# Key sums of a linear-attention and mixture-of-experts kernel: the halves of the key products added on GpSimd, 16 transposed blocks in place of 32, and other slots for the steps

## The reference

```
x = x + layernorm(attn(layernorm(x)))
x = x + layernorm(ffn(layernorm(x)))

def attn(x):                       # 16 heads of 16
    xn = rms(x, g1)
    Q, K, V = xn @ Wq.T, xn @ Wk.T, xn @ Wv.T
    pQ, pK = elu(Q), elu(K)
    Q1, Q2 = split(pQ, 2);  K1, K2 = split(pK, 2)
    kv1 = einsum('bshe,bshd->bsed', K1, V) * SCALE     # sum over the 16 HEADS of one position
    kv2 = einsum('bshe,bshd->bsed', K2, V) * SCALE
    attn = Q1 kv1 - lmb * Q2 kv2
    attn = (1 - LAMBDA_INIT) * rms(attn, g2)
    attn = rms(attn, g3) + attn
    return gelu(attn @ W1.T) @ W2.T + attn

def ffn(h):                        # 16 query heads, 4 key heads, causal softmax attention, RoPE
    h = h + softmax_attention(rms(h)) @ Wo ; clip
    top 2 of 8 experts by softmax(rms(h) @ Wr), each silu(h Wg) * (h Wu) @ Wd, width 512
    clip(h + weighted sum of the experts)
```

## Time and profile before

| | us |
|---|---|
| median of 3 runs | 3368.0 |
| lowest, highest | 3363.05, 3370.25 |
| profiled execution, its own time | 3372.2 |
| its span | 3370.3 |
| busy: TensorE, VectorE, ScalarE, GpSimd | 2875.5, 2161.4, 1670.3, 1732.7 |

### The profile page before, as it was taken

How to read it: one execution, slowest core, us unless ns; L and a number is a source line. 1 busy time by engine, 2 the same in 40 slices (tenths; PEclk the granted TensorE clock), 3 DMA queues, 4 the chain that set the end, 5 groups by cost and what they waited for, 6 DMA issues and landing times. The chain is left out here.

```text
span 3370.3 us, 54068 instructions
## 1 busy us (share of the span) xinstructions
PE 2875.5 (85%) x17348; PEld 1707.3 (51%) x17349; DVE 2161.4 (64%) x4652; ACT 1670.3 (50%) x3836; POOL 1732.7 (51%) x2301
## 2 busy tenths in 40 slices
PE   4566899899989889989988998988759999999990
PEld 3344545554545554554555454443336666666650
DVE  3566887888898888888888888667322222222226
ACT  1234657667657656666765765765412222222224
POOL 5686746765765865776676575241212222222221
PEclk8788999999999999999999999999779999999995
DMA  1000000000000000000000000002243333333326
GB/s 46 0 10 10 11 9 14 14 25 12 27 22 14 28 20 17 22 19 23 17 22 27 12 24 19 12 25 81 73 112 53 57 58 57 58 52 58 58 43 200
DMA packets 102670, 123.21 MB, mean 37 GB/s; under 512 B 14384, under 2 KB 90160, under 8 KB 102448
## 3 DMA queue, kind: packets, MB, share of 16 engines
q1 hardware_dynamic: 76720, 85.54, 8.6%
q0 software_dynamic: 25728, 34.88, 6.0%
HBM read 58.23 MB, written 61.36 MB: 35 GB/s over the span
## 5 line engine op out<-in xcount | busy, mean ns | idle before, releaser
L822 ACT ACTIVATE wd<-SP_ 128x512 f32<-128x512 f32 (+3 forms) x1536 | 722.9, 488 | 477.9 <-PE SP_ L1439 334.0
L1105 DVE TENSOR_REDUCE NM<-MX 128x1 f32<-128x512 f32 (+3 forms) x1216 | 763.6, 655 | 243.9 <-PE MX L1396 145.2
L1393 PE MATMUL MX<-KST,QST 96*128 96x512 bf16 (+3 forms) x1536 | 457.5, 336 | 101.5 <-DVE NM L1105 89.2
L509 POOL TENSOR_TENSOR wg<-wu 128x1024 f32<-128x1024 f32 x256 | 487.4, 1924 | 106.3 <-DVE wu L941 106.2
L1436 PE MATMUL SP_<-QST,KST 99*128 99x512 bf16 (+3 forms) x1536 | 500.9, 333 | 34.3 <-ACT wd L822 15.8
L1718 POOL DMA_INDIRECT scratch_h<-Y,XG x136 | 211.2, 1553 | 604.5 <-DVE Y L1781 511.1
L1759 DVE TENSOR_TENSOR AG<-UB,SL 128x512 f32<-128x512 f32 x136 | 94.1, 692 | 460.3 <-PE UB L1798 456.9
L1736 ACT ACTIVATE SL<-GB 128x512 f32<-128x512 f32 x136 | 81.2, 597 | 603.4 <-PE GB L1798 603.4
L954 DVE TENSOR_TENSOR wg<-wu,SUM 128x1024 f32<-128x1024 f32 x256 | 310.4, 1213 | 99.7 <-PE SUM L1290 99.7
L1393 PEld LDWEIGHTS MX<-KST,QST 96*128 96x128 bf16 x1536 | 135.7, 98 | 433.9 <-DVE NM L1105 303.5
L1453 PE MATMUL OA<-wd,V 128*32 128x512 f32 (+3 forms) x3072 | 332.7, 506 | 1.0 <-ACT wd L822 0.4
(11 more groups left out here) (244 smaller groups left out, 4974.0 us busy)
## 6 DMA issues: line engine op xcount, KB each, us to landing
XG<-scratch_xs SPq DMA_DIRECT2D x136, 130.0 KB, 2.1
wu<-in_L_attn_x SPq DMA_DIRECT2D x64, 128.0 KB, 2.1
scratch_x<-wu SPq DMA_DIRECT2D x64, 128.0 KB, 1.7
scratch_h<-H SPq DMA_DIRECT2D x64, 128.0 KB, 1.7
X<-scratch_x SPq DMA_DIRECT2D x16, 512.0 KB, 4.0
HH<-scratch_h SPq DMA_DIRECT2D x16, 512.0 KB, 4.8
out<-X SPq DMA_DIRECT2D x16, 512.0 KB, 3.2
wg<-in_L_ffn_Wg SPq DMA_DIRECT2D x8, 512.0 KB
```

The costliest lines, as they stand in the source:

```text
L509: sg["prod1"].by(pool.tensor_tensor(P1[:, k // 2, (k % 2) * hh * D:(k % 2 + 1) * hh * D].rearrange("p (h e d) -> p h e d", h=hh, e=HD), QK ...
L822: sg["exp"].by(act.activation(PR[:, n % 8, q0:512], SP_[:, n % 2, q0:512], ACT.Exp))
L1105: sg["mx"].by(dve.tensor_reduce(NM[:, u % 2, part, i, h:h + heads], MX[:, index % 2, 0:heads * n].rearrange("p (h n) -> p h n", n=n), AX.X ...
L1393: m = pe.matmul(out[:, k], QST[0:MROW, j % 2, g * G + h + k, i * P:(i + 1) * P], KST[0:MROW, keys % RK, g, 0:n], start=k == 0, stop=not la ...
```

## The change

GpSimd adds the two quarters of each half of P1 in place as soon as both are there: the second 1024 floats are added to the first 1024. TensorE then has 4 heads' worth of blocks per half, 16 blocks per tile. The count `prod1` goes up by 6 per tile, not 4, and its users follow. Beside this many steps stand in other slots, the scatters are tied to slots 7, 15, 20 and to slot 2 of the next period, and LATE and AHEAD of the short units are 2.2 and 7.9 in place of 2.5 and 9.2. `share` and `LAST_BACK` are written in another way and give the same numbers.

```diff
-        LATE, AHEAD, DONE, SPREAD = (2.5, 1.6), (9.2, 6.2), (2.0, 3.0), (3.5, 8.5)
+        LATE, AHEAD, DONE, SPREAD = (2.2, 1.6), (7.9, 6.2), (2.0, 3.0), (3.5, 8.5)
...
@@ SyncE
-                        if i == 4 and p >= 0 and have(p + 3):
-                            load(p + 3)
-                        if i == 14 and have(p - 17):
-                            t = p - 17
+                        if i == 4 and have(p - 18):
+                            t = p - 18
...
-                        if i == 19 and have(p - 6):
+                        if i == 21 and have(p - 6):
...
+                        if i == 21 and have(p + 3):
+                            load(p + 3)
...
@@ GpSimd, key_products
+                    if k % 2 == 1:
+                        need("prod1", 6 * t + 3 * (k // 2) + 2)
+                        half = P1[:, k // 2]
+                        sg["prod1"].by(pool.tensor_tensor(half[:, 0:hh * D], half[:, 0:hh * D], half[:, hh * D:2 * hh * D], ALU.add))
...
+                def spread(k, n):
+                    t = CH * (k // CH) + 2 * (k % CH) + n // 2
+                    scatter(t, n % 2)
...
@@ GpSimd, the table
-                        if i == 2 and have(p - 1):
+                        if i == 1 and have(p - 1):
                             head_roots(p - 1)
...
+                        if i == 15 and have(p + 2):
+                            x_coefficients(p + 2)
...
-                        if i == 19 and have(p + 2):
-                            x_coefficients(p + 2)
...
@@ VectorE
-                        if i == 21 and (p - 21) % CH == 0 and have(p - 21):
-                            choose((p - 21) // CH)
+                        if i == 0 and (p - 22) % CH == 0 and have(p - 22):
+                            choose((p - 22) // CH)
...
@@ TensorE, sum_heads
-                    need("prod1", 4 * t + 2 + 2 * half)
-                    hh = H // 2
+                    need("prod1", 6 * t + 3 + 3 * half)
+                    hh = H // 4
```

## The result

The changed kernel takes 3497.6 us in the median of four runs (3495.4 to 3499.8), the kernel before 3367.4 on the same chip: a ratio of 1.039, interval 1.0373 to 1.0406. That is 130 us slower, and above the range of 3280 to 3385. The profiled execution has a span of 3497.9 us, 127.6 more than before.

A forecast was written before the change was run, and what follows sets the result against it. TensorE's own queue, with VectorE close behind, was taken to bound the steady part, and GpSimd the part before 290 us. Steady -51 and early +24 gave -27 us: 3341 us on the median, 0.8% faster, range 3280 to 3385.

The forecast's parts named there:

- Where GpSimd idles more than 4.44 us per stretch the work lies beside TensorE's: Steady part: two additions per tile, 4.44 us, cost nothing where GpSimd has that much idle time in a stretch.
- The addition's price: On GpSimd: one addition of 1024 elements takes 2.22 us, between 1.92 and 2.89, so 4.44 us per tile.
- the slower rival: GpSimd leads with additions of 2.9 us; early and tight stretches lengthen, steady gain halves to 25: 3398 us, chance 0.21.
- The tight three stretches: Neighbouring stretches, 828.4 to 918.5 us, where GpSimd would take the lead: 89.3 us against 90.1, counted as 0.
- The five others of the round: Steady stretches outside the tight three: TensorE's 1.80 us per tile returned nine tenths in long ones, half where VectorE is nearly full.
- The early part: Cycles before 290 us, where GpSimd sets the pace: 9 us lost in the first six, 15 in the next five, +24.
- The blocks' saving: On TensorE: 16 of 32 transposes per tile removed, 1.80 us per tile; 51 us counted in the steady part.
- VectorE's hold: VectorE instructions held up by GpSimd's additions: 43 us on VectorE, of which 8 would show, left inside the range.
- The 0.33 us taken from the head norm: Hold per addition on one VectorE instruction, read from the head norm's 411 ns at least and 744 ns median.
- The moves: Steps put in other slots, mostly swaps of independent neighbours: counted as 0, plus or minus 1 us per stretch.
- VectorE becomes the bound: Rival: TensorE's saving turns into longer waits for VectorE's maxima and the gain is cancelled: 3368 us, chance 0.14.

## Why the prediction was wrong

In medians (to the nearest microsecond) the change comes apart as +36 for the slots (3368 to 3404), -60 for the 16 blocks (3404 to 3344, with short additions) and +154 for the additions (3344 to 3498). The forecast had 0, about -51 to -94, and +24. The split holds in this order only: in the old slots additions and blocks together are +138 and the slots then -8.

**The step that failed** is "Where GpSimd idles more than 4.44 us per stretch the work lies beside TensorE's". Idle time was read as slack. It consists of waits at fixed places of a queue worked off in order, and an instruction put elsewhere in the queue doesn't fill them: it delays what stands behind it. 36 additions in the idlest stretches made the kernel 23 us slower, and with all 128 of them 126 of the 154 us stay when fills stand in their place. How the 23 us divide between the queue and the hold at the router is not shown. The prediction named who waits behind the second addition (ScalarE's normalization, TensorE's second block) and then gave them no price; the page shows it, 28.1 to 50.2 us of idle time at the normalization.

**The addition's price** was right (2.38 against 2.22), and so was the count of 128. Two of them are 4.75 us, just over the 4.7 from which the slower rival was said to decide.

**The tight three stretches** were given 0: they lost 7.6 us per round, 38 in five. The five others of the round were given gains of 1.6 or 0.9 us each and lost 7.7 together. Both fit the reason above.

**The early part:** +24 was forecast, +40 came, up to tile 12. The six first cycles lost 16.4 instead of 9: the second addition stands directly ahead of the blocks that need it, and the 8 blocks behind it run at the lower clock, 1.97 us where the sum had 1.3. From the first key product (101.21 us) to the end of these blocks (116.93) it is 15.7 us, 14.7 in the sum. GpSimd's window from 212.2 to 264.7 shows two cycles of 26.2 us on average against 24.7 forecast and 21.75 before, with GpSimd busy 48.5 of 52.5 us and waiting 1.2. There it does set the pace, as forecast; where the further 1.5 us of a cycle come from was not traced:

```profile
212.20:238.10 25.90, 12.90 (x44) 8.95 (x43) 16.18 (x21) 6.68 (x17) 23.68 (x28) 0.63 0.03 11
238.10:264.70 26.60, 15.71 (x64) 10.97 (x63) 16.80 (x22) 9.97 (x22) 24.78 (x31) 0.63 0.04 10
```

**The blocks' saving** was in the right range, 37 to 60 us by the two runs, and the larger only where no full additions make TensorE wait. The clock is not the reason for that difference: with the additions it is 0.946 with 32 blocks and 0.947 with 16 (tiles 23 to 63). Of 14.4 us less work per round 7.8 came back there as longer idle time of TensorE (37.7 to 45.5); without full additions 3.1 of 12.1 did (29.0 to 32.1).

**VectorE's hold** had no term, only 8 us left to the range; it is worth about 28 us beyond what a fill does. The 0.33 us taken from the head norm was the wrong row: its busy time stayed (40.4 us before, 40.2 after; the median fell from 744 to 458 ns), and the additions hold three others, by up to 2.2 us each. Here the Trainium skill's "SBUF — State Buffer", section "SBUF: two separate sides", cited as a rule that speaks against the change, was nearer: the pair of ports belongs to whichever instruction started first, for its whole length. The trace agrees: the residual's addition on VectorE, 0.42 us in the median before, takes up to 2.59 beside additions of 2.35.

**The moves** were given 0, plus or minus 1 us per stretch: by themselves they cost 36, nearly all of it in the scatters and the router's step; beside the additions they cost nothing (3506 and 3498).

**The rivals.** The slower one had the right place in its second condition ("where GpSimd's queue after the second addition makes TensorE wait in the long stretches too") and the wrong price, 30 against 130, because it still counted a gain of 25 in the steady part and took the delays only where GpSimd is full. "VectorE becomes the bound" did not come: TensorE's wait for the maxima went from 11.6 to 14.5 us, under the 20 that were named as the sign.

**What stays open.** How the 126 us of occupied queue divide between late coefficients, late sums and the lower clock: no run separates them, and the waits feed each other. Of the hold of 28 us some 5 may be the router's, within the noise; which of the two others, the residual's or the rotation's, has the rest was not run. Nor was `choose` moved without the scatters.

## What to carry to other kernels

Idle time of an engine that works off its queue in order is not free room. Before work is put on it, list what stands behind the new instruction, who waits for that, and how long each wait is already; price the delay there at the full length of the instruction, and take it off only where the waiter has proven slack. List beside it what another engine does at the same time and may be held. Where several engines wait for each other in turn, 15 idle microseconds of a stretch of 40 prove nothing. A trial of the addition in its idlest stretches alone would have told the sign at once. And a schedule that is tuned to one set of durations is a part of the change: test it alone.

## What the runs showed of the hardware

Two streams of 1024 floats added in place on GpSimd take 2.38 us, the product with repeated inputs of as many 1.93.

A VectorE instruction on 4 columns with one input in SBUF takes 0.17 us alone, 0.88 in the median beside a GpSimd fill that reads nothing and 2.24 beside a GpSimd addition. Of VectorE's instructions with two inputs in SBUF, the residual's addition was held by up to 2.2 us beside additions, and beside fills no more than in the kernel before (median 426 ns and at most 1334; 424 and 1499 before):

```profile
L1018 DVE TENSOR_TENSOR wu<-wu x64: 401/426/1334, 204.6 to 2349.3; 128x256 f32<-128x256 f32 x64
```

The Trainium skill's "SBUF — State Buffer", section "SBUF: two separate sides", names two classes: a VectorE instruction with two SBUF inputs is locked out only by a GpSimd instruction that reads SBUF, one in a two-port mode by any. The medians of the residual's addition agree with the first. The 4-column instruction behaves like the second, which was not expected of one so small; in which mode it ran no row shows.

TensorE's granted clock follows its own waits here: 0.99 in a round before, 0.95 after, with 26 and 47 us of idle time, and 0.73 in place of 0.64 where extra matmuls filled its waits. Behind a wait of 2.92 us it stood at the lower of its two levels, and eight transposes took 1.76 us to the start of the next instruction, where sixteen took 1.80 at the higher level.
